# Cross-attention with routed experts: paired padding writes, 20 first tiles, idle products, merged PSUM steps and an earlier second norm

## The reference, cut to what matters

```python
x = x + xattn(layernorm(x), ctx)      # x: 16 batches of 256 tokens of 256; ctx: 77 keys of 192 for a batch
x = x + ffn(layernorm(x))             # 8 experts, each token goes to its best 2

# xattn: 16 heads of 64; q, k, v and the output projection each with a low-rank part added to their weights
#   73 keys have one softmax, the last 4 keys ("ipa") a second one with weights of their own; both are added
out = softmax(q @ k.T / 8) @ v + softmax(q @ k_ipa.T / 8) @ v_ipa

# ffn
top_logits, top_idx = top_k(x @ gate_w, 2)
y = sum(softmax(top_logits)[e] * (silu(x @ w1[e]) @ w2[e]) for e in top_idx)
```

## Time and profile before

| what | us |
|---|---|
| runs | 745.17, 741.42, 741.09 (median 741.42) |
| the profiled execution | 745.7, its span 743.7 |
| setup, up to the first body's scores | 67 |
| one batch of the loop | 26.53 |
| from the last batch's scores to the first product of the experts | about 37 |
| one tile of the experts | 5.69 |

### The profile page before, as it was taken

One profiled execution on the slowest core, in us unless ns is written; L12 is line 12 of the kernel. 1 busy time (PEld: TensorE's weight loads), 2 busy tenths in 40 slices (PEclk: granted clock), 3 DMA queues, 4 the chain that ended last, 5 costly groups with the idle time before them and its releaser, 6 DMA issues.

```text
span 743.7 us, 22841 instructions
## 1 busy us (share of the span) xinstructions
PE 674.2 (91%) x7980; PEld 560.0 (75%) x7981; DVE 548.5 (74%) x1239; ACT 455.4 (61%) x768; POOL 495.5 (67%) x582
## 2 busy tenths in 40 slices
PE   6637799999999999999999999779979999999994
PEld 2226688788778878878877887568869888888993
DVE  3953778898898898889889889875737555555552
ACT  1435878778777877877877787544624344434441
POOL 3115546877887887788778788765666656665665
PEclk9997999999999999999999999899989999999998
DMA  9911101211211112121121121133655654454550
GB/s 268 321 48 47 31 21 34 75 33 46 76 38 52 62 45 62 46 74 33 46 76 43 47 63 48 42 99 77 147 132 103 96 91 85 80 90 80 94 79 1
DMA packets 51558, 56.35 MB, mean 76 GB/s; under 512 B 15104, under 2 KB 45824, under 8 KB 51520
## 3 DMA queue, kind: packets, MB, share of 16 engines
q1 hardware_dynamic: 37136, 38.50, 18.1%
q0 software_dynamic: 14384, 17.33, 13.4%
HBM read 30.67 MB, written 25.76 MB: 76 GB/s over the span
## 4 chain that ended last, share of the span: by engine, by line
PE 52%; DVE 17%; issue 10%; SPq 6%; DMA 5%; ACT 5%; POOL 4%; POOLq 1%; DVEq 0%
PE ps L1532 37%; PE ps L1650 5%; DVE pt_s L1268 4%; PE ps L1630 4%; DVE sm L1338 3%; DVE q_s L1268 2%; PE ps L1705 2%; PE ps L529 2%; DVE v_s L1268 2%; POOL out_x L499 2%; DMA out_x<-pt_s,token_of 2%; ACT q_s L1062 1%; DVE x_sb L1363 1%; PE ps L1563 1%; DMA pt_s<-in_wo 1%
## 5 line engine op out<-in xcount | busy, mean ns | idle before, releaser
L499 POOL DMA_INDIRECT out_x<-pt_s,token_of x78 | 124.9, 1601 | 28.4 <-issue 27.2
L588 ACT ACTIVATE q_s<-ps 128x512 f32<-128x512 f32 x78 | 46.5, 596 | 126.9 <-PE ps L1532 123.1
L715 DVE TENSOR_TENSOR wq_s<-q_s,wq_s 128x512 f16<-128x512 f32 x78 | 55.8, 718 | 80.5 <-ACT wq_s L592 65.7
L1532 PE MATMUL ps<-q_s,ffnw 128*128 128x256 f16 x936 | 110.7, 276 | 1.1 <-DVE q_s L697 1.1
L1532 PE MATMUL ps<-ffnw,wq_s 128*128 x936 | 109.1, 273 | 0.1
L894 POOL TENSOR_TENSOR prob<-prob,mx 128x1168 f32<-128x1168 f32 x64 | 77.6, 1234 | 37.8 <-DVE mx L1331 37.8
L1532 PEld LDWEIGHTS ps<-ffnw,wq_s 128*128 128x128 f16 x936 | 89.8, 98 | 14.2 <-issue 2.6
L1532 PEld LDWEIGHTS ps<-q_s,ffnw 128*128 x936 | 91.0, 99 | 12.4 <-issue 1.5
L1532 PE MATMUL ps<-xt_s,wq_s 128*128 128x256 f16 x768 | 90.2, 279 | 1.9 <-DVE xt_s L1268 1.9
L1532 PE MATMUL ps<-wo_s,ot_s 128*128 128x256 f16 x768 | 89.4, 273 | 1.4 <-DVE ot_s L1268 1.4
L1532 PEld LDWEIGHTS ps<-xt_s,wq_s 128*128 128x128 f16 x768 | 76.8, 100 | 13.0 <-issue 1.9
(11 more groups left out here) (210 smaller groups left out, 1230.5 us busy)
## 6 DMA issues: line engine op xcount, KB each, us to landing
prob<-rows_dram SPq DMA_DIRECT2D x39, 264.0 KB
wstage<-in_ffn_w SPq DMA_DIRECT2D x16, 512.0 KB, 3.6
x_sb<-in_x SPq DMA_DIRECT2D x4, 1024.0 KB, 10.7
out_x<-x_sb SPq DMA_DIRECT2D x16, 256.0 KB
rows_dram<-wstage SPq DMA_DIRECT2D x8, 264.0 KB
out_x<-pt_s,token_of POOLq DMA_INDIRECT x78
pt_s<-in_wq SPq DMA_DIRECT2D x2, 512.0 KB, 4.6
pt_s<-in_wo SPq DMA_DIRECT2D x2, 512.0 KB, 8.3
```

The source lines that it names most:

```text
L499: pool.indirect_dma_start(out_rows, bass.IndirectOffsetOnAxis(ap=token_of[:, j % UNROLL, c:c + 1], axis=0), y_sb[:, j % UNROLL, c, :], Non ...
L588: act.activation(h32[:, half, :], h_ps(t, j, half), ACT.Silu, scale=1 / WSCALE).then_inc(silu_done, 1)
L715: dve.tensor_tensor(hs[:, j % 2, 1, 2 * half:2 * half + 2, :].rearrange("p f n -> p (f n)"), h32[:, half, :], hs[:, j % 2, 0, 2 * half:2 * ...
L1532: last = pe.matmul(o, lhs(a, n), rhs(c, n), start=(i == 0), stop=(i == len(steps) - 1))
```

## The change

- **Padding writes.** `fill_up` issues two of the eight writes after each of the tiles 3, 7, 11 and 15, in place of all eight after tile 3.
- **20 first tiles.** `EARLY` goes from 16 to 20, so that one more block of four is written out and the wait `all_there` stands behind tile 15. `late_table` is cut in two; the second part (`late_rest`) runs after tile 11.
- **Merged steps.** The query quarters 0 and 1 (banks 6 and 7) leave PSUM in one ACT and one DVE instruction of 1,024 columns; the same for the two value halves (banks 1 and 2).
- **The second norm earlier.** In the bodies 1 to 14 POOL runs `rstd_2` between the first `scatter` and `normalise(b, 1)`; ACT runs `normalise_2` between `pt(b, 1)` and `pt(b, 2)` and `x2t_copy` after `pt(b, 5)`; PE runs `transpose_2` between the probability transposes 5 and 6 and `router` before attend 1. The banks of attend 1 and attend 2 are swapped (4, 6, 5, 7).
- **Idle products.** PE runs 12, 10 and 6 products of 512 columns whose results nobody reads: in the last body ahead of its probability transposes, ahead of the last projection, and behind it.

```diff
-EARLY = 16
+EARLY = 20
...
+        def values_banks():
+            return ps[0:ORG, 1:3, :].rearrange("p c n -> p (c n)")
+        def queries_pair():
+            return ps[:, 6:8, :].rearrange("p c n -> p (c n)")
...
-            return ps[:, 4 + k, :]
+            return ps[:, (4, 6, 5, 7)[k], :]
...
             def fill_up(t):
-                if t != UNROLL - 1:
+                if t < UNROLL - 1 or t >= 5 * UNROLL - 1:
                     return
-                sp.wait_ge(pad_made, 5)
-                sp.wait_ge(tab_done, 2)
-                for e in range(EXPERTS):
+                if t == UNROLL - 1:
+                    sp.wait_ge(pad_made, 5)
+                    sp.wait_ge(tab_done, 2)
+                pair = (t - UNROLL + 1) // UNROLL * 2
+                for e in (pair, pair + 1):
                     r = sp.value_load(pads[0:1, e:e + 1], min_val=0, max_val=EXPERTS * REGION - RT)
...
                 link(dve.tensor_reduce(all_row_of[:, 0:LATE], past_n_late, AX, ALU.add))
+            def late_rest():
+                flags = (past_late, past_n_late)
                 link(dve.scalar_tensor_tensor(out=all_row_of[:, 0:LATE], in0=tnum[:, 0:LATE], scalar=float(RT),
...
                 normalise(b, 0)
                 if routed and not last:
                     scatter(b - 2, 0)
+                if not first and not last:
+                    rstd_2(b - 1)
                 normalise(b, 1)
-                if not first:
+                if last:
                     rstd_2(b - 1)
...
+            def q_pair(b):
+                act.wait_ge(q_mm, 4 * b + 2)
+                act.activation(q_s[:, 0, 0:4, :].rearrange("p m n -> p (m n)"), queries_pair(), ACT.Copy,
+                               scale=1 / WSCALE).then_inc(q_hi, 2)
+            def v(b):
+                hi_of(v_s[0:ORG, 0, :], values_banks(), 1 / WSCALE, v_mm, b + 1, v_hi)
...
                 if not last:
-                    q(b + 1, 0)
-                    q(b + 1, 1)
+                    q_pair(b + 1)
                 exp(b, 1)
...
                 pt(b, 0)
                 pt(b, 1)
+                if not first and not last:
+                    normalise_2(b - 1)
                 pt(b, 2)
...
                 pt(b, 4)
+                if last:
+                    normalise_2(b - 1)
                 pt(b, 5)
-                if not first:
-                    normalise_2(b - 1)
+                if not first and not last:
+                    x2t_copy(b - 1)
...
+            def q_pair(b):
+                dve.wait_ge(q_hi, 4 * b + 2)
+                dve.scalar_tensor_tensor(
+                    out=q_s[:, 1, 0:4, :].rearrange("p m n -> p (m n)"), in0=queries_pair(), scalar=1 / WSCALE,
+                    in1=q_s[:, 0, 0:4, :].rearrange("p m n -> p (m n)"), op0=ALU.mult, op1=ALU.subtract
+                ).then_inc(q_split, 2)
...
                 if not last:
-                    q(b + 1, 0)
-                    q(b + 1, 1)
+                    q_pair(b + 1)
                 if not first:
                     residual(b - 1)
...
+                if t == 11:
+                    late_rest()
...
+            def keep_warm(bank, count):
+                for i in range(count):
+                    pe.matmul(ps[:, bank, :], wq_s[:, 0, 0, 0:P], wq_s[:, 0, 1, 0:512], start=True, stop=True)
...
                 new_values(b)
+                if last:
+                    keep_warm(0, 12)
...
                 transpose_probs(b, 5)
+                if not first and not last:
+                    pe.wait_ge(pt_split, 8 * b + 2)
+                    transpose_2(b - 1)
                 pe.wait_ge(pt_split, 8 * b + 3)
                 transpose_probs(b, 6)
...
                     if k == 1 and not first and not last:
-                        transpose_2(b - 1)
-                    if k == 2 and not first and not last:
                         pe.wait_ge(k_split, 2 * b + 4)
                         router(b - 1)
...
             transpose_2(BATCH - 2)
+            keep_warm(0, 10)
             project(BATCH - 1, 0)
             pe.wait_ge(slots, BATCH - 1)
             router(BATCH - 2)
             project(BATCH - 1, 1)
+            keep_warm(0, 6)
```

More of the change, by code:

```diff
@@ L686, in late_table @@
                 adds(adds_all[:, EARLY:NT], EARLY, LATE, all_starts[:, 0:LATE]).then_inc(tab_done, 1)
-            return full_tiles, early_table, all_rows, late_table
+            return full_tiles, early_table, all_rows, late_table, late_rest
         def ffn_dve(dve, then, late_table):
@@ L964, in body @@
                     scatter(b - 2, 0)
+                if not first and not last:
+                    rstd_2(b - 1)
                 normalise(b, 1)
-                if not first:
+                if last:
                     rstd_2(b - 1)
-                if last:
                     scatter(b - 2, 0)
@@ L1092, in put_kipa @@
                 last.then_inc(kipa_put, 1)
-            def v(b, k):
-                hi_of(v_s[0:ORG, 0, k * 512:k * 512 + 512], values_bank(k)[0:ORG, :], 1 / WSCALE, v_mm,
-                      b + 1, v_hi)
+            def q_pair(b):
[4 more added lines that the diff above has]
+                hi_of(v_s[0:ORG, 0, :], values_banks(), 1 / WSCALE, v_mm, b + 1, v_hi)
             def copy_scores(b, t):
@@ L1162, in body @@
                     q(b + 1, 3)
-                v(b, 0)
-                v(b, 1)
+                v(b)
                 if first:
@@ L1181, in body @@
                 ot(b, 0)
-                if not first and not last:
-                    x2t_copy(b - 1)
                 ot(b, 1)
@@ L1317, in k_, with v @@
                 last.then_inc(k_split, 1)
-            def v(b, k):
-                lo_of(v_s[0:ORG, 1, k * 512:k * 512 + 512], values_bank(k)[0:ORG, :], 1 / WSCALE,
-                      v_s[0:ORG, 0, k * 512:k * 512 + 512], v_hi, 2 * b + k + 1, v_split)
+            def q_pair(b):
[4 more added lines that the diff above has]
+                ).then_inc(q_split, 2)
+            def v(b):
+                lo_of(v_s[0:ORG, 1, :], values_banks(), 1 / WSCALE, v_s[0:ORG, 0, :], v_hi, b + 1, v_split)
             def keys(t):
@@ L1427, in place_rows @@
                 assert c.n == ROUTE, c.n
-            full_tiles, early_table, all_rows, late_table = tile_tables(dve)
+            full_tiles, early_table, all_rows, late_table, late_rest = tile_tables(dve)
             def body(b, first, last):
@@ L1764, in body @@
                     new_keys(b + 1)
-                pe.wait_ge(v_split, 2 * b + 2)
+                pe.wait_ge(v_split, b + 1)
                 transpose_probs(b, 4)
```

## The result

The change does not make the kernel faster. In 20 runs each the changed kernel has a median of 746.72 us (743.48 to 749.64), the kernel before 744.46 (741.09 to 748.19); the ratio is 1.0037, with a 95% interval of 1.002 to 1.0053. I had 735.8, in a range of 729 to 741.5. Of the 10.9 us between, 3.0 lie in the base: the forecast starts from the median of three runs, 741.42, and that of twenty is 744.46. The profiled execution took 747.66 us (span 745.9), against 745.7 (743.7).

The account below looks back on a forecast made before the run. PE was taken as nearly full. Padding -6.6, loop 0.0, last body +0.2 and idle products +0.3 sum to -6.1 us: 735.3 from the 741.42 median, set at 735.8 for a possibly smaller pause; 8-in-10 range 729 to 741.5.

Parts of the forecast that it names:

- the last sentence on the loop: ACT's last two head copies 0.2 us later; PE waits for them only in the last body, +0.2 once.
- The rest of the loop: 14 like batches: attend 0 at +0.92, PE's reordering -0.9, DVE and POOL meeting within 0.05; sum 0.0 us a batch.
- The padding term: Expert tiles: spread padding writes remove PE's one pause, a 6.98 us loss from a late load and lower clock; -6.6 us.
- 20 first tiles and late_rest: Expert tiles behind the pause: PE is idle only 0.07 of 181 us, so nothing to gain; 0.
- Merged steps: Query and value copies from PSUM: value merge saves DVE 0.05 us, query merge starts `residual` 0.97 later.
- Idle products: Last batch: twelve fall into idle PE, ten and six hide behind the first tiles' load except a rest; +0.3 us.
- The loop loses: Rival, chance 0.14: transposes 4 wait for POOL's `normalise(b, 1)` in every batch; no gain from +0.44 a batch, 739 to 746.
- Less to gain at the pause: Rival, chance 0.18: pause among the tiles costs only 4.0 or 2.7 us, or last pair lands late, costing 2.6; 738 to 739.

Follow-up runs that it names:

- experiment 3: The changed kernel with ACT's copy of the router's row (`row_high`) moved between the first and second head copy: ratio 0.9997.
- experiment 7: The changed kernel with the row copy between the first two head copies and the first two query quarters separate again: ratio 0.9874.
- 10: As experiment 7, with POOL's first scatter split, one transfer ahead of the norm factor and second normalise, the others behind: 726.47 us, ratio 0.9795.
- experiment 9: The kernel before with only the eight padding writes spread three, three and two, behind tiles 3, 7 and 11: ratio 0.996.
- 11: As 10, but with 16 first tiles and the padding writes three, three and two: 728.20 us, ratio 0.9811.
- experiment 6: The changed kernel without its 28 idle products: ratio 1.0049.

## Why the prediction was wrong

**The step that failed** is the last sentence on the loop: "ACT's last two head copies come some 0.2 later because `row_high` gets between; where no x is transposed ahead of the projection (last body) PE has to wait for them: +0.2 once." The place was right and the size nearly so, but there was no cover. I took the x transposes (0.5) as hiding the delay in the 14 bodies, without working out when head copy 3 would be done on DVE. In the changed kernel it is done 0.15 after them, and with its start up the projection is 0.30 late in each of the 13 bodies: 3.8 of the loop's 4.8 us, shown by experiment 3. The last body of the kernel before could have told it. There PE waits 0.45 for the same head copy with no x transposes in between, and starts 466.75 - 465.26 = 1.49 after the scores, no later than with them (1.48):

```profile
465.26 1.03 PE L1630 MATMUL ps<-k_s,q_s 64*128 64x77 f16 x48
466.75 2.79 PE L1532 MATMUL ps<-wo_s,ot_s 128*128 128x256 f16 x24 [0.45 <-DVE ot_s L1268]
```

So the copy came just as the transposes would have ended, and any delay had to show in whole. In the last body of the changed kernel the wait is 0.74, so the delay is 0.29 where I had 0.2:

```profile
473.71 2.79 PE L1556 MATMUL ps<-wo_s,ot_s 128*128 128x256 f16 x24 [0.74 <-DVE ot_s L1286]
```

**The rest of the loop held.** Without that wait the body is 26.57, beside 26.53 predicted from the first profile (attend 0 came at +1.03 where I had +0.92; behind it 3.85 where I had 3.96). That POOL binds behind DVE was right too, but not that they meet within 0.05: experiment 7 frees DVE and finds POOL 0.36 earlier, 10 frees both and gains 1.06. The base moved: against the shorter rhythm of the kernel before, 0.28 a body more, because the 0.26 us ahead of the router that the change was to save are not there.

**The padding term was mis-sized**: -4.2 in the changed kernel, -3.4 to -6.4 in the nine kernels with these edits (231.6 less 228.2 to 225.2), where I had -6.6. The pause itself gave 6.7 of its 7.15; the small gaps took up to 3 back, and why they vary is open. I had argued that PE is idle for 0.07 of 181 us behind the pause, and took it that this would hold without the pause. Behind tile 15 no load was late in the changed kernel (SP waited 2.2 for the last write). Where it landed late, in experiment 9 after 5.39, it cost PE some 0.65; by my sum, 1.17 + 2.65 + 5.39 - 5.69 less the slack of 1.5, it would have been 2.0.

**20 first tiles and late_rest** were put at 0, and 11 beside 10 bears that out: 728.20 and 726.47 us, the intervals of the ratios overlap.

**Merged steps.** The values gave what their row said: 1.21 for one DVE step of 1,024 columns, in place of 1.27 for two.

In a body of experiment 7, which has the same merged values:

```profile
346.23 1.21 DVE L1287 SCALAR_TENSOR_TENSOR v_s<-ps,v_s 73x1024 f16<-73x1024 f32 x1
```

The 0.125 us that I had worked out from the Trainium skill (VectorE: DVE Perf Modes, the TRN2 errata) does not show: 0.06 does. The query pair is the part that costs.

**Idle products** were put at +0.3. Within the changed kernel they give 1.7 at the first expert product; against the kernel before, which has no slow product there, no cost of them shows: from the last scores to the first expert product, where I had +0.5 with the last body's 0.2, it is 36.25 us after and 36.59 before. I had looked at the transposes, which POOL holds; I did not look at the first expert product, which also follows a wait of PE. The Trainium skill (TensorE: Matmul & The Clock Gate, Part 1) says that an idle array is throttled and that activity releases it; the granted clocks of experiment 6, 0.50 and 1.00, agree.

**The rivals.** "The loop loses" has the right sign and size (0.34 a body, 0.58 against the shorter rhythm) at the wrong place: I named POOL's second normalise. The 0.34 is also the upper edge of what I had given a body, +0.35. "Less to gain at the pause" came true as well, by gaps, not by the clock. Each I had priced for itself, and the two together lie outside my range. The setup's +1.9 is in no step. All of it lies ahead of the first scores (67.25 us before, 69.21 after), in code that the diff leaves as it was; the scores of the second body lie between 93.7 and 99.1 us in ten profiles of the changed attention, and between 93.5 and 95.3 in four of the old one. Whether that is the change or the execution is open.

## What to carry to other kernels

When a product moves ahead of another on a full engine, follow each copy that the pushed-back product releases, through every instruction queued with it, up to the next wait of the full engine, and work that out in clock times for the repeated body, not only for the odd one at the end. A merged step saves little where instructions in a row already overlap, and it delays its first half by the wait for its second. Profile the kernel before twice: a wait that you mean to save may not be there in the next execution.

## What the runs showed of the hardware beyond that

- The same loop code ran at 26.53 us a body in one execution and at 26.29 in another, each through the bodies 2 to 13; the difference sits in one head copy of ACT, 1.19 to 1.28 us after the start of the product that releases it in the one, 0.89 in the other. In the other twelve profiles, whatever the kernel, it is 0.89 too.
- Among the tiles PE's weight loads have 4 to 14 gaps in 100 us (540 to 640) with no wait that the profile shows, of 0.8 us at most, in sum 1.2 to 4.6 us: over code run in loops, in one-pass blocks or in one line, with 16 first tiles or 20, and, fewest in sum, in the kernel before.
- With 12 products on data that nobody uses ahead of them, the last batch's transposes ran at a granted clock of 1.00 (2.4 GHz) through waits of 1.98 and 1.36 us; without them it was 0.50 (1.2 GHz) behind a wait of 4.67, and the 32 transposes took 6.19 in place of twice 1.94. It does not hold each time: of eight profiles with the products one, that of experiment 7, has 0.50 at the first of these transposes too; the 32 take 5.32 behind a wait of 2.22.
